# A gated cross-attention and mixture-of-experts kernel: order of the prologue, places of the routing picks, and the conditions under which scatters wait

## The reference

```python
x = x + tanh(g_xattn) * xattn(layernorm(x), ctx)
x = x + tanh(g_ffn) * ffn(layernorm(x))
# xattn: q = ln(x) @ Wq (16 heads of 64); k, v = ln(ctx) @ Wkv (one head shared by all)
#        softmax(q k^T / 8) v @ Wo  +  (silu(gate) * h) @ Wff2,  with h, gate = ln(x) @ Wff1
# ffn:   silu(x @ sh_up + b) @ sh_down + b
#        + sum over the 2 best of 8 experts of weight * (silu(x @ up_e + b_e) @ down_e + b_e)
```

## Time and profile before

| | |
|---|---|
| median of 3 runs | 538.68 us |
| profiled execution, its own time | 537.07 us |
| span of its instructions | 535.3 us |
| TensorE busy | 494.9 us (92%) |
| VectorE, ScalarE, GpSimd busy | 406.2, 327.2, 291.4 us |
| mean granted TensorE clock | 0.986 |

### The profile page before, as it was taken

How to read it: one execution, slowest core, us unless ns; L and a number is a source line. 1 busy time by engine, 2 the same in 40 slices (tenths; PEclk the granted TensorE clock), 3 DMA queues, 4 the chain that set the end, 5 groups by cost and what they waited for, 6 DMA issues and landing times.

```text
span 535.3 us, 13844 instructions
## 1 busy us (share of the span) xinstructions
PE 494.9 (92%) x4026; PEld 480.3 (90%) x4026; DVE 406.2 (76%) x1251; ACT 327.2 (61%) x1092; POOL 291.4 (54%) x334
## 2 busy tenths in 40 slices
PE   7779999999999999999999999999999979999940
PEld 7769999999999999999999999999987869999930
DVE  7687778688887878878788878687777887888830
ACT  3667566756675767566567565756667526767730
POOL 3588636444543755364355436444686334677773
PEclk9999999999999999999999999999999999999995
DMA  5660300121003010200301030023598955778753
GB/s 173 197 223 12 99 2 32 31 81 60 21 20 118 31 30 25 103 32 20 118 21 32 8 120 29 10 79 100 182 335 321 414 194 120 128 136 143 120 65 39
DMA packets 40212, 53.85 MB, mean 101 GB/s; under 512 B 4597, under 2 KB 34218, under 8 KB 39146
## 3 DMA queue, kind: packets, MB, share of 16 engines
q1 hardware_dynamic: 31856, 41.48, 23.8%
q0 software_dynamic: 8000, 11.86, 11.5%
q10 hardware_dynamic: 314, 0.01, 0.1%
HBM read 28.15 MB, written 25.21 MB: 100 GB/s over the span
## 4 chain that ended last, share of the span: by engine, by line
PE 62%; DVE 13%; issue 7%; DMA 6%; ACT 5%; POOLq 3%; POOL 2%; SPq 0%; DVEq 0%; ACTq 0%
PE bank L1548 12%; PE bank L1550 11%; PE bank L1549 11%; PE bank L1629 5%; PE bank L1641 4%; PE bank L1734 4%; DMA out_x<-norm_probs,th 4%; PE bank L1724 4%; POOLq L733 3%; PE bank L1645 3%; PE bank L1632 2%; PE bank L1739 2%; PE bank L1563 2%; DVE norm_probs L1016 2%; ACT norm_probs L822 2%
## 5 line engine op out<-in xcount | busy, mean ns | idle before, releaser
L627 POOL TENSOR_TENSOR norm_probs<-norm_probs,rden 128x512 f32<-128x512 f32 x64 | 66.6, 1041 | 101.2 <-DVE rden L1196 100.7
L1548 PE MATMUL bank<-acts,weights 128*128 128x256 f32 x384 | 109.3, 285 | 4.7 <-POOL weights L598 4.7
L1549 PE MATMUL bank<-acts,weights 128*128 128x256 f32 x384 | 108.0, 281 | 0.0
L1550 PE MATMUL bank<-acts,weights 128*128 128x256 f32 x384 | 107.8, 281 | 0.0
L822 ACT ACTIVATE norm_probs<-bank,nmax 128x128 f32<-128x128 f32 x256 | 90.6, 368 | 24.0 <-DVE nmax L1152 23.9
L632 POOL TENSOR_TENSOR acts<-uf,acts 128x256 fp32r<-128x256 f32 x64 | 47.5, 743 | 68.7 <-ACT acts L810 68.7
L1548 PEld LDWEIGHTS bank<-acts,weights 128*128 128x128 f32 x384 | 72.6, 189 | 5.7 <-issue 4.4
L746 POOL DMA_INDIRECT out_x<-norm_probs,th x39 | 60.7, 1557 | 28.0 <-DMA out_x<-norm_probs,th 13.2
L1550 PEld LDWEIGHTS bank<-acts,weights 128*128 128x128 f32 x384 | 72.5, 189 | 0.0
L1549 PEld LDWEIGHTS bank<-acts,weights 128*128 128x128 f32 x384 | 72.3, 188 | 0.0
L810 ACT ACTIVATE acts<-uf 128x256 fp32r<-128x256 f32 x64 | 26.8, 419 | 61.1 <-DVE uf L1221 61.0
(11 more groups left out here) (252 smaller groups left out, 1545.3 us busy)
## 6 DMA issues: line engine op xcount, KB each, us to landing
parked<-stage SPq DMA_DIRECT2D x12, 512.0 KB, 3.5
weights<-parked SPq DMA_DIRECT2D x6, 1024.0 KB, 9.8
slot_rows<-tf SPq DMA_DIRECT2D x8, 680.0 KB, 6.5
spare<-slot_rows SPq DMA_DIRECT2D x39, 136.0 KB
ct<-in_ctx SPq DMA_DIRECT2D x8, 256.0 KB, 2.7
xs<-in_x SPq DMA_DIRECT2D x8, 256.0 KB, 4.8
stage<-in_L_ffn_up_w SPq DMA_DIRECT2D x8, 256.0 KB, 2.8
stage<-in_L_ffn_down_w SPq DMA_DIRECT2D x8, 256.0 KB, 3.1
```

The costliest lines, as they stand in the source:

```text
L627: pool.tensor_tensor(pr[:, s % 2], pr[:, s % 2], rden[:, s % 2, :].unsqueeze(2).broadcast_to((P, 4, P)), ALU.mult).then_inc(probs_ready, 1)
L1548: pe.matmul(ps, wts[1], mov[0], start=first, stop=False, skip_group_check=True)
L1549: pe.matmul(ps, wts[0], mov[0], start=False, stop=False, skip_group_check=True)
L1550: return pe.matmul(ps, wts[0], mov[1], start=False, stop=last, skip_group_check=True)
```

## The change

It has five parts.

- Weights of the prologue: the first queries wait for the first half (columns 0 to 511) of each Wq chunk only, and queries of pair 2 for the rest. VectorE splits chunk 1 in two pieces, the second after the values. The high part of wkv moves to ScalarE, its low part on VectorE behind the context's transposes. Chunk 6 is loaded and split before chunk 5, its low part is VectorE's, chunk 5 moves into unit 0. TensorE waits for chunk 4 a quarter at a time.
- Group 0, unit 0: tanh, the gated products and the high part of the hidden slice are taken before or around the first exponentials; the gate's weight parts move from the prologue to after them.
- Between groups and tiles: the low parts of step 3 go from GpSimd to VectorE, ahead of the window table; `shared_down(3)` and `add_shared(2)` no longer wait for that table.
- Picks of tiles 0 and 1 are made at steps -2 and -1, that of tile 2 at step 0; SP additionally waits for the transposes of tiles 0 and 1 before it reuses their buffers.
- Scatters: the wait for t - 3 becomes conditional like the others, with a third value and a third `value_load` per tile; the wait for t - 4 is unconditional. For it VectorE keeps a third count (`hist[2]`), the tables have seven margins instead of three, and the rows of padding name four distinct ranges of output rows in turn instead of three.

The diff, cut to its core (the definitions of `hidden_high`, `hidden_tanh`, `hidden_values`, `gate_parts` and `key_weights` hold the instructions that stood in line before; the tables' arithmetic and the places of small tensors are left out):

```diff
-EARLY = 6
 CHUNK_SLOT = {0: [6], 1: [7], 2: [8], 3: [9], 4: [10]}
-LO_ON_POOL = (2, 4, 5, 6, 7, 8, 9, 10)
+LO_ON_POOL = (2, 4, 5, 7, 8, 9, 10)
+HI_ORDER = (1, 2, 3, 4, 6, 5, 7, 8, 9, 10)
+LO_PARTS = {1: 2, 2: 2, 4: 4}
...
+        def split(eng, n, part=None):
+            if n >= NCA:
+                eng.wait_ge(ring_ready, n - NCA + 1)
+            else:
+                eng.wait_ge(chunk_split_done[n], LO_PARTS.get(n, 1) if part is None else part)
...
-            for n in range(NCA):
+            for n in range(5):
                 load_chunk(n)
-                if n == EARLY - 1:
-                    load_ctx(1)
-                    load_x(1)
+            load_chunk(6)
+            load_ctx(1)
+            load_x(1)
+            load_chunk(5)
+            for n in range(7, NCA):
...
+                src = pad_row[:, D:ROW] if k % 4 == 3 else pad_pairs[k % 4].rearrange("p e k -> p (e k)")
+                sp.dma_start(pads[:, k, D:ROW], src).then_inc(pads_stored, 16)
...
+                    if t < 6:
+                        sp.wait_ge(gT_filled, t - 3)
...
-                pool.wait_ge(chunk_hi_done, n)
+                pool.wait_ge(chunk_hi_done, HI_ORDER.index(n) + 1)
                 for i in range(4):
                     src_i, hi_i, lo_i = [t[:, i] if len(t.shape) == 3 else t[:, 256 * i:256 * i + 256] for t in (src, hi, lo)]
                     done = pool.tensor_tensor(lo_i, src_i, hi_i.bitcast(F32), ALU.subtract)
-                done.then_inc(chunk_split_done[n], 1)
+                    if (i + 1) % (4 // LO_PARTS.get(n, 1)) == 0:
+                        done.then_inc(chunk_split_done[n], 1)
...
+                    if first and s == 0:
+                        split_lo(5)
...
-            for m in range(KT):
-                step = TPS - 1
-                pool.wait_ge(hh_done, step * KT + m + 1)
-                pool.tensor_tensor(hh[:, step % 2, 1, m, :], hf[:, step % 2, m, :], hh[:, step % 2, 0, m, :].bitcast(F32),
-                                   ALU.subtract).then_inc(last_h_ready, 1)
...
-                    due_1, due_2 = [pool.value_load(turns[t:t + 1, i:i + 1], min_val=0, max_val=16) for i in range(2)]
+                    due_1, due_2, due_3 = [pool.value_load(turns[t:t + 1, i:i + 1], min_val=0, max_val=16) for i in range(3)]
+                if t >= 4:
+                    pool.wait_ge(y_added[t % 4], 16 * (t // 4) + 16)
                 if t >= 3:
-                    pool.wait_ge(y_added[(t - 3) % 4], 16 * ((t - 3) // 4) + 32)
+                    pool.wait_ge(y_added[(t - 3) % 4], due_3 + (16 * ((t - 3) // 4) + 16))
...
-                    if 1 <= s <= NU:
-                        act.wait_ge(mix_freed, mix_index(f"FF{s - 1}", g, first, last) + 1)
-                        if not (first and s < 3):
-                            act.wait_ge(ff2_done, u - 2)
-                        act.activation(uT[0][:, (s - 1) % 2, :], uf[:, :], ACT.Copy).then_inc(uh_done, 1)
+                    if 1 <= s <= NU and not (first and s == 1):
+                        hidden_high(s - 1, g, first, last)
+                    if first and s == 0:
+                        hidden_tanh(s, g, first, last)
...
+                    if first and s == 0:
+                        hidden_high(s, g, first, last)
                     if first:
-                        for n in CHUNK_SLOT.get(s, []):
+                        for n in [5] if s == 0 else CHUNK_SLOT.get(s, []):
...
-            split_hi(5)
+            split_hi(6)
...
+            landed(act, 0)
+            act.activation(wkv[0][:, :, :], stage[:, 0, 0:KT * P].rearrange("p (k n) -> p k n", k=KT), ACT.Copy
+                           ).then_inc(kv_hi_done, 1)
...
-            early_lo(1)
+            early_lo(1, 0)
...
+            key_weights()
+            first_lo(cnT, 2, cnT_ready)
...
+            early_lo(1, 1)
...
+                    if first and s == 0:
+                        hidden_values(s)
...
+                        early_lo(6)
+                        gate_parts()
...
+                    counts_so_far(2)
...
+            hidden_lo(TPS - 1)
             window_table()
+            add_shared(2)
             dve.wait_ge(tables_done, 2)
             experts_of = dve.value_load(window[0:1, 0:1])
-            add_shared(2)
...
+                if t in (-2, -1):
+                    dve.wait_ge(gathered[t + 2], 16)
+                    pick_meta(t + 2, t + 2)
...
-                if t == 0:
-                    pick_meta(0, 0)
-                    pick_meta(1, 1)
                 if t == 1:
-                    pick_meta(2, 2)
                     turn_table()
-                if t >= 1 and runs(t + 2):
+                if t >= 0 and runs(t + 2):
...
+                if first and pair == 2:
+                    split(pe, 1)
+                    split(pe, 2)
...
-            split(pe, 1)
-            split(pe, 2)
+            split(pe, 1, 1)
+            split(pe, 2, 1)
...
-                if j < TPS - 1:
-                    pe.wait_ge(h_ready, KT * j + KT)
-                else:
-                    pe.wait_ge(last_h_ready, KT)
+                pe.wait_ge(h_ready, KT * j + KT)
...
+            shared_down(3)
             pe.wait_ge(tables_done, 2)
             experts_of = pe.value_load(window[0:1, 0:1])
-            shared_down(3)
```

More of the change, by code:

```diff
@@ L205, in program @@
         weight = route(4).rearrange("p (t c) -> p t c", t=2)
[L206 to L207 removed]
+        hist_t = route(3 * NE).rearrange("p (k e) -> p k e", k=3)
+        hist = [hist_t[:, k, :] for k in range(3)]
         weight8 = routing[:, 0:4 * NE].rearrange("p (t c e) -> p t c e", t=2, c=2)
@@ L243, in program @@
         upto = consts[:, 306:306 + NE * NE].rearrange("p (e f) -> p e f", e=NE)
[L244 to L247, removed]
+        slow_table = slow_stage[:, 0:7 * 16].rearrange("p (k e) -> p k e", k=14)
+        margin, due = slow_table[:, 0:7], slow_table[:, 7:14]
+        floor, opens = [slow_stage[:, 128 + 24 * i:152 + 24 * i].rearrange("p (k e) -> p k e", k=3) for i in range(2)]
+        two_before = consts[:, 284:285]
         tile_past = consts[:, 450:458]
@@ L250, in program @@
         shares = consts[:, 486:486 + WIN_TILES]
-        late_early = consts[:, 494:494 + 2 * NE].rearrange("p (k e) -> p k e", k=2)
-        late, early = [late_early[:, k, :] for k in range(2)]
+        missing = consts[:, 386:386 + 3 * NE].rearrange("p (k e) -> p k e", k=3)
         meta = th[:, 0:2 * TILES].rearrange("p (t n) -> p t n", n=2)
@@ L682, in iteration @@
                         expert_lo(s - 4)
-                    if first:
+                    if first and s > 0:
                         for n in CHUNK_SLOT.get(s, []):
@@ L800, in probs_hi, with hidden_high, hidden_tanh @@
                 act.activation(pT[0][:, :], t_ps[:, :], ACT.Copy).then_inc(pTh_done, 1)
+            def hidden_high(s, g, first, last):
+                u = g * NU + s
+                act.wait_ge(mix_freed, mix_index(f"FF{s}", g, first, last) + 1)
+                if not (first and s < 2):
+                    act.wait_ge(ff2_done, u - 1)
+                act.activation(uT[0][:, s % 2, :], uf[:, :], ACT.Copy).then_inc(uh_done, 1)
+            def hidden_tanh(s, g, first, last):
+                u = g * NU + s
+                b = mix_ps[mix_bank(f"FF{s}", g, first, last)]
+                act.wait_ge(mix_filled, mix_index(f"FF{s}", g, first, last) + 1)
+                if not (first and s == 0):
+                    act.wait_ge(u1_done, u)
+                act.activation(th[:, :], b[:, GT:2 * GT], ACT.Tanh, scale=0.5).then_inc(tanh_done, 1)
             def iteration(g, first=False, last=False):
@@ L831, in iteration @@
                         probs_hi(u - 1, first and s == 1)
[L832 to L837, removed]
+                    if s < NU and not (first and s == 0):
+                        hidden_tanh(s, g, first, last)
                     if s in PARK_STEPS and not first and not last:
@@ L1143, in small_steps, with hidden_values @@
                     at_step += 1
+                def hidden_values(s):
+                    u = g * NU + s
+                    b = mix_ps[mix_bank(f"FF{s}", g, first, last)]
+                    dve.wait_ge(tanh_done, u + 1)
+                    dve.scalar_tensor_tensor(u1[:, :], th[:, :], 1.0, b[:, GT:2 * GT], ALU.add, ALU.mult
+                                             ).then_inc(u1_done, 1)
+                    if s in (1, 2, 3):
+                        small_steps(1)
+                    if s == 6 and not first:
+                        hot_choices(g - 1)
+                    dve.wait_ge(u1_done, u + 1)
+                    if not (first and s == 0):
+                        dve.wait_ge(u_ready, u)
+                    dve.scalar_tensor_tensor(uf[:, :], b[:, 0:GT], 0.5, u1[:, :], ALU.mult, ALU.mult
+                                             ).then_inc(mix_freed, 1)
                 for s in range(NU + 2):
@@ L1359, in window_shares @@
```

(9 more changed lines are left out.)

87 lines of the change are left out of this document (40 added, 47 removed).

## The result

The changed kernel takes 554.15 us (median of 4 runs, 552.52 to 555.71), the kernel before 538.00 (4 runs, 537.16 to 539.99): a ratio of 1.028, 95% interval [1.0228, 1.0334]. The forecast was 555.5. The profiled execution took 553.46 us (before: 537.07), so it holds +16.4, beside a forecast of +16.9.

The account below looks back on a forecast made before the run. GpSimd's sequencer in the scatter loop was taken as the bound; -2.4 - 1.0 + 0.2 + 20.1 = +16.9 us on the profiled 537.07 gave 554.0, 555.6 by the median. Predicted: 555.5, range 547 to 564.

Parts of the forecast that it names:

- The bound: Scatter loop: GpSimd's sequencer instructions, about 1.82 us a round, pace it and set the end, not TensorE or landings.
- The scatter loop, +20.1: 38 rounds at 0.63 us for load and register wait, 23.9, less 1.0 and 2.8 of waits; bounds +14.5 to +26.4.
- Start of the prologue, -2.1: TensorE's first product at 14.1 instead of 16.24, after two of GpSimd's four Wq pieces: 2.1 us earlier.
- Second unit, -2.4 at its maxima: Prologue: second unit gains 0.3 us beyond the 2.1; sum -2.4, bounds -5.6 to +1.
- the gate's weight parts: VectorE ahead of the second unit's maxima: these parts, moved out of the prologue, were priced at 0.5 us.
- TensorE waits at the first attend instead.: Prologue: TensorE's idle before 29.05 and 32.58 loses its causes, and it waits at the first `attend`; no size given.
- Rival C: Scatter stage: full ring makes TensorE wait, its clock falls and it paces some 20 tiles: +22, about 577; chance 0.03.
- Between groups and tiles, -1.0: Before the first tiles: TensorE idles go, VectorE's added low parts cost; first result 1.0 us sooner, bounds -3 and +1.
- +0.2 in the last group: Last group: a smaller `counts_so_far` costs 0.2 us.
- The signs: 114 loads, spacing 2.5 to 2.7 in all rounds, copies waiting from about the twentieth, TensorE share about 0.7, clock 1.00.
- Rival A: Scatter loop: the third load costs nothing and landings were the bound; 534.5 us, faster; chance 0.10.
- B: Scatter loop: the third load overlaps in part, 0.3 us a round; total about 543; chance 0.05.

Follow-up runs that it names:

- experiment 1: Change with the old scatter waits (two loads per tile): 534.31 us; kernel before with one more unused load per tile: 556.89; with two more: 575.91.
- experiment 4: Change with flags packed into one load per tile: two flags and the unconditional wait at distance three, 532.32 us; all three flags, 529.97, again 530.35.
- the 20 products: 20 overwritten identity products on TensorE ahead of the first attended values; two-load change 534.38 us with, 534.20 without; three flags in one load 529.98 with.
- Experiment 2: Kernel before with one part added: shared_down(3) ahead of the window table, its low parts on VectorE, 539.91 us; or the earlier picks alone, 536.21.
- the shared part alone: Kernel before with shared_down(3) ahead of the window table and its low parts on VectorE instead of GpSimd: 539.91 us, ratio 1.0026.
- experiments 1 and 3: Both ran the change with the old scatter waits (two loads): 534.31 us, later 534.20; the second also added 20 identity products: 533.95, later 534.38.

## Why the prediction was right, step by step

- **The bound.** Right for what is added: each load lengthens the loop (experiment 1). I had not seen the floor of 1.85 from scatter to scatter, just above the sequencer's 1.82: taking instructions out of the kernel before gains next to nothing (experiment 4).
- **The scatter loop, +20.1.** Measured +19.95. The parts: 18.3 is the load (0.48 a round, where its rows add to 0.55); the other 1.7 is the register wait less what the altered waits gave back, which no run separates. My rows add to 23.9, so 4.0 did not appear, where I had given back 3.8. The size is right, the reason only in part: long rounds of before took in some of the load, but the step from three to four loads, with the two waits long covered, is no larger (0.45 on the mean, 0.53 on the shortest round).
- **Start of the prologue, -2.1.** First product at 14.25 instead of 16.24, -2.0. Right, for the reason given: TensorE starts when GpSimd's second piece is done.
- **Second unit, -2.4 at its maxima.** Only -1.2: they come at 28.27, where I had said 27.1. The term mis-sized is the one of the gate's weight parts, for which I took 0.5 us. VectorE's timeline of the changed kernel shows 1.7:

```profile
24.08 1.19 DVE L1100 TENSOR_TENSOR weights<-spare,weights 128x1024 fp32r<-128x1024 f32 x1
25.19 1.01 DVE L1104 CAST gate_t<-cols 128x16 fp32r<-128x16 f32 x1
26.24 0.65 DVE L1106 TENSOR_TENSOR gate_t<-cols,gate_t 128x16 fp32r<-128x16 f32 x1
```

  They are 16 columns wide, yet take 1.01 and 0.65; in the kernel before, at 15.90 and 16.21, the same two took 0.27 and 0.17. Here they lie beside two GpSimd instructions and end within 0.05 us of them:

```profile
24.24 1.93 POOL L636 TENSOR_TENSOR norm_probs<-norm_probs,rden 128x512 f32<-128x512 f32 x1 [0.64 <-DVE rden L1246]
26.13 0.72 POOL L641 TENSOR_TENSOR acts<-uf,acts 128x256 fp32r<-128x256 f32 x1
```

- **"TensorE waits at the first attend instead."** Right, and it had a consequence that I did not see: 2.93 us of idle time, and with it a clock at 1.2 GHz for 3.4 us. Between the maxima of unit 1 and those of unit 8 it is 45.3 to 45.4 us in the four executions with one such drop in between (46.3 with one of double length) and 44.2 to 44.3 in the three with the products, as before: 1.1 us more. Together: -2.4 forecast, -1.2 reached, -0.1 left at the ninth unit's maxima (73.79 before, 73.69 after). But the profiled execution of before is a lucky one: in the four others with its prologue (experiments 1 and 2) the clock fell near the first products, in one of them a second time, and these maxima came at 74.6 to 75.2. In the six with the changed prologue and without the 20 products they came at 73.6 to 74.8. So the prologue brings more than the 0.1 of this pair, some 0.7 at the medians of these executions.
- **Rival C** was wrong where it was put. With the ring full, TensorE's share falls to 0.73 and the clock stays at 1.00 (window as above):

```profile
488.00:524.00 36.00, 26.30 (x194) 23.10 (x194) 20.13 (x58) 19.19 (x51) 21.70 (x15) 1.00 0.55 80
```

  The clock fell in the prologue instead, at 32.8, behind the first 16.2 us that I had taken as evidence. The Trainium skill (TensorE: Matmul & The Clock Gate, "A second HAM failure mode: psum-queue depth-cycling") tells of frequent short idles between groups of matmuls that make the clock swing. The trace shows such idles in the full-ring stretch without any swing, and in the prologue one drop behind one long idle, so it does not bear that pattern out here.
- **Between groups and tiles, -1.0, and +0.2 in the last group.** The second is right: from -0.1 at the ninth unit to +0.1 at the last scatter of routed rows (427.22 and 427.33). The first is -3.5 (19.70 to 16.20 us): mis-sized by 2.5, and past my bound of -3. The earlier picks alone bring -2.3. I had put the price of VectorE's two extra low parts (1.3) at full; but with GpSimd's subtractions gone, its window table runs at full speed. The same instructions, before and after:

```profile
428.70 1.12 DVE L1424 TENSOR_TENSOR ct<-tf,routing 128x56 f32<-128x56 f32 x1
429.86 0.21 DVE L1426 TENSOR_REDUCE ct<-ct 128x8 f32<-128x56 f32 x1
430.11 0.90 DVE L1427 TENSOR_TENSOR ct<-ct,tf 128x8 f32<-128x8 f32 x1
```

```profile
430.10 0.21 DVE L1466 TENSOR_TENSOR ct<-tf,routing 128x56 f32<-128x56 f32 x1
430.34 0.21 DVE L1468 TENSOR_REDUCE ct<-ct 128x8 f32<-128x56 f32 x1
430.59 0.17 DVE L1469 TENSOR_TENSOR ct<-ct,tf 128x8 f32<-128x8 f32 x1
```

  That is 1.6 us less in two small instructions. They had lain beside GpSimd's two subtractions (L723, 2.52 us from 428.47) and ended within 0.1 us of the end of each. Experiment 2 isolates this: with the picks alone, GpSimd's subtractions stay and the two take 1.11 and 0.90; with the shared part alone they are gone, and it is 0.21 and 0.17. The Trainium skill (SBUF — State Buffer, "SBUF: two separate sides") says that GpSimd shares one pair of ports with VectorE instructions of some kinds, among them those with two inputs in SBUF while GpSimd reads SBUF too, and that whoever starts first holds it for its whole instruction while the other stands still. The trace agrees, with 1.12 beside GpSimd and 0.21 alone for an instruction with two inputs, and 0.21 both times for the reduction, which has one.
- **What the errors did.** In the profiled pair the prologue was forecast 2.3 too good and the stretch before the tiles 2.5 too poor: they cancelled by luck, and the total came out within 1.4 us because the one large term was right. The medians of experiments 1 and 3 put the change without its third load 4.6 to 5.4 us below the kernel before, which is more than the 3.4 by which the loop starts sooner in this pair.
- **The signs.** 114 loads, the copies' waits from the 23rd on and a share of 0.73 at a clock of 1.00 came as forecast, though over the whole stage of 72 us the share is still 0.93. The spacing was not 2.5 to 2.7 in all rounds but in 21 of 38; the others run from 2.36 to 3.19.
- **Rival A** (534.5) and **B** (543) are excluded by experiment 1. One thing in A was true: waits for landings do stand behind the sequencer's work. Those at distance three are worth 2.4 us of loop in the one pair of executions that shows them (experiment 4), not what the releasers' names suggest.

## What to carry to other kernels

Before you replace a wait by a conditional one, count the sequencer's instructions in a round of that loop: here a flag loaded from memory cost 0.45 to 0.48 us in each of 38 rounds, to spare a wait worth some 2.4 us in all once the loads are few, and with no gain to be seen while they are three (a loop of 98.59 against 96.90). If the condition is worth having, pack all flags of a round into one word and take them apart in registers. And price a two-input instruction of VectorE by what GpSimd does beside it, not by its size.

## What the hardware showed that I had not expected

- A scatter by GpSimd (128 rows of 256) starts no sooner than 1.85 us after the one before, with 1.55 of its own, also where the sequencer was ready sooner (28 of 38 rounds at 1.85 to 1.86 with one load, and 1.87 where the sequencer's rounds took 1.38).
- Two-input VectorE instructions of 8 and 56 columns took 0.90 and 1.12 us beside a GpSimd subtraction and 0.17 and 0.21 without one; a reduction of 56 columns took 0.21 both times. But a one-input copy of 16 columns that also changes the type took 1.01 beside GpSimd and 0.27 in the kernel before, so one input alone does not make an instruction safe.
- One idle stretch of 2.93 us, among shorter ones, was followed by 3.4 us at 1.2 GHz and a loss of 1.1 us; drops of the same length or twice it turned up in other executions at other places (between 15.8 and 21.2 us in four executions with the prologue of before, between 435 and 450 us in six executions of all kinds).
